# Attention values, their copies and exponentials by pairs of units, and batch 3's first steps two slots later

## What is computed

```
x = x + ssm(layernorm(x))          # conv, SiLU, decay/drive, scan over time, projection
x = x + ffn(layernorm(x))          # 8 experts of 512, all of them for each token
x = x + attention(layernorm(x))    # 16 heads of 8
x = x + ffn(layernorm(x))          # the same ffn again

# ffn
g = einsum('bsh,ehf->ebsf', x, w_gate);  u = einsum('bsh,ehf->ebsf', x, w_up)
h = silu(g) * u
out = einsum('ebsh,bse->bsh', einsum('ebsf,efh->ebsh', h, w_down), cw)

# attention: a row sees its own chunk of 10 and 25 tokens to the left
scores = einsum('bhsd,bhtd->bhst', q, k) + mask
out = einsum('bhst,bhtd->bhsd', softmax(scores), v)
```

## Time and profile before

| | us |
|---|---|
| median of 3 runs | 1425.51 (1422.82 to 1425.74) |
| profiled execution, its own time | 1425.63 |
| its span, first to last instruction | 1423.8 |
| PE busy | 1364.1 |
| DVE, ACT, POOL busy | 951.1, 773.1, 517.1 |

### The profile page before, as it was taken

How to read it: one execution, slowest core, us unless ns; L and a number is a source line. 1 busy time by engine, 2 the same in 40 slices (tenths; PEclk the granted TensorE clock), 3 DMA queues, 4 the chain that set the end, 5 groups by cost and what they waited for, 6 DMA issues and landing times.

```text
span 1423.8 us, 31460 instructions
## 1 busy us (share of the span) xinstructions
PE 1364.1 (96%) x12700; PEld 1179.9 (83%) x12700; DVE 951.1 (67%) x2294; ACT 773.1 (54%) x1049; POOL 517.1 (36%) x517
## 2 busy tenths in 40 slices
PE   4889999999999999999999989999999999999998
PEld 3788777888888888887888878888888888888887
DVE  6766777775876668568675676757856675576543
ACT  6565648653565556637475665556634563365321
POOL 4260564533423453247312751236503421341000
PEclk9999999999999999999999999999999999999999
DMA  6210231003010310131003300050003000300000
GB/s 233 59 31 17 67 79 32 20 12 78 2 47 16 71 24 1 47 68 35 9 2 83 64 2 9 1 116 32 2 1 73 8 2 1 71 9 2 9 1 8
DMA packets 70235, 51.39 MB, mean 36 GB/s; under 512 B 4140, under 2 KB 60508, under 8 KB 70092
## 3 DMA queue, kind: packets, MB, share of 16 engines
q1 hardware_dynamic: 70060, 49.38, 14.4%
q10 hardware_dynamic: 32, 0.02, 0.0%
HBM read 44.92 MB, written 4.46 MB: 35 GB/s over the span
## 4 chain that ended last, share of the span: by engine, by line
PE 79%; DVE 8%; POOL 5%; issue 4%; ACT 3%; DMA 0%; DVEq 0%; POOLq 0%
PE pd L1125 26%; PE pg L289 8%; PE pu L289 7%; PE pg L291 7%; PE pg L290 7%; PE pu L290 7%; PE pu L291 7%; PE att_ps L766 2%; POOL arena L713 2%; PE att_ps L791 2%; DVE h L1234 1%; POOL arena L715 1%; PE pd L1117 1%; DVE x L1222 1%; PE side_ps L326 1%
## 5 line engine op out<-in xcount | busy, mean ns | idle before, releaser
L1185 ACT ACTIVATE h<-pg 128x512 f32<-128x512 f32 x512 | 304.3, 598 | 601.8 <-PE pg L291 599.6
L1125 PEld LDWEIGHTS pd<-w_down,h 128*128 128x128 f32 x3840 | 483.4, 192 | 33.9 <-issue 4.1
L1125 PE MATMUL pd<-w_down,h 128*128 128x128 f32 x3840 | 489.7, 276 | 1.3 <-DVE x L1222 1.1
L1234 DVE TENSOR_TENSOR h<-h,pu 128x512 f32<-128x512 f32 x512 | 344.8, 678 | 214.9 <-PE pu L291 204.8
L289 PE MATMUL pg<-ffn_x_hi,w_gate_hi 128*128 128x512 f32 (+1 forms) x544 | 248.3, 456 | 1.1 <-DVE ffn_x_lo L376 1.1
L289 PE MATMUL pu<-ffn_x_hi,w_up_hi 128*128 128x512 f32 (+1 forms) x544 | 210.3, 387 | 12.6 <-DVE h L1234 12.5
L290 PE MATMUL pu<-ffn_x_lo,w_up_hi 128*128 128x512 f32 (+1 forms) x544 | 208.4, 383 | 0.0
L291 PE MATMUL pg<-ffn_x_hi,w_gate_lo 128*128 128x512 f32 (+1 forms) x544 | 208.3, 383 | 0.0
L290 PE MATMUL pg<-ffn_x_lo,w_gate_hi 128*128 128x512 f32 (+1 forms) x544 | 208.2, 383 | 0.0
L291 PE MATMUL pu<-ffn_x_hi,w_up_lo 128*128 128x512 f32 (+1 forms) x544 | 207.9, 382 | 0.0
L976 POOL TENSOR_TENSOR att_arena<-att_arena,r_sums 128x512 f32<-128x512 f32 (+1 forms) x72 | 72.6, 1008 | 272.9 <-DVE r_sums L856 272.8
(11 more groups left out here) (222 smaller groups left out, 1440.1 us busy)
## 6 DMA issues: line engine op xcount, KB each, us to landing
arena<-bc_spread SPq DMA_DIRECT2D x56, 256.0 KB, 4.6
att_arena<-v_rows SPq DMA_DIRECT2D x64, 144.0 KB, 3.9
att_arena<-v_rows SPq DMA_DIRECT2D x64, 128.0 KB, 3.7
arena<-in_x SPq DMA_DIRECT2D x8, 256.0 KB, 3.1
x<-in_x SPq DMA_DIRECT2D x8, 256.0 KB, 3.5
w_down<-in_w_down SPq DMA_DIRECT2D x8, 256.0 KB, 5.0
v_rows<-att_arena SPq DMA_DIRECT2D x8, 256.0 KB, 2.3
out<-x SPq DMA_DIRECT2D x8, 256.0 KB, 2.2
```

What stands on the lines that cost most here:

```text
L1125: last = nc.tensor.matmul(pd[:, t * P:(t + 1) * P], h_b[:, d % NH, t * P:(t + 1) * P], wd[:, d % NCH, :], start=d % CPE == 0 and t == 0, s ...
L1185: nc.scalar.activation(h_b[:, c % NH, :], pg[c % 2][:, :], ACT.Silu).then_inc(gate_done, 1)
L1234: nc.vector.tensor_tensor(h, h, pu[d % 2][:, :], ALU.mult).then_inc(h_done, 1)
```

## The change

The attention of a batch goes by pairs of units from the exponentials on. A new function `Att.pair(j, n, part)` gives the slot of a step: the pair's first unit plus a part of its own for even and odd units; in the last pair, of one unit, the part is scaled by 0.75.

- PE: `values(m)` has all windows of a pair in one block, in one bank, and stands behind the scores of the next pair.
- ACT: one Exp over 1024 columns for a pair.
- DVE: masks, maxima, sums and transposes are still one for each unit, but both units' follow one another or lie close; the copy to `attT` is one for a pair, 120 columns instead of 60. `smax` and `rsum` get a second buffer.
- POOL: subtractions and multiplications likewise; `like_heads` does parts 0, 1 in pair 0 and parts 2, 3 in pair 1.
- Batch 3's `st`, `rows`, `ln` and `win` are two slots later; batch 1's `y` moves from 23.1 to 23.5.

```diff
-        return dict(st=-25.2, rows=-24.2, ln=-22, win=0.7, dt=7.7, k=(10.7, 13.7, 16.4, 19.1), y=23.1)
+        return dict(st=-25.2, rows=-24.2, ln=-22, win=0.7, dt=7.7, k=(10.7, 13.7, 16.4, 19.1), y=23.5)
...
-    return dict(st=o - 11, rows=o - 9.5, ln=o - 9, win=o - 6.5, dt=o + 1, k=(o + 10, o + 16, o + 26, o + 32), y=o + 42)
+    s = 2 if i == 3 else 0
+    return dict(st=o - 11 + s, rows=o - 9.5 + s, ln=o - 9 + s, win=o - 6.5 + s, dt=o + 1, k=(o + 10, o + 16, o + 26, o + 32), y=o + 42)
...
-S_SC, S_MASK, S_MASK1, S_MAX, S_SUM, S_TURN, S_VAL, S_OUT, S_Q = 1 / 8, 1 / 4, 5 / 8, 3 / 8, 1 / 8, 5 / 8, 7 / 8, 1, 3 / 8
+S_SC, S_MASK, S_MAX, S_SUB, S_EXP, S_SUM, S_NORM, S_TURN, S_VAL, S_OUT, S_Q = \
+    -0.125, (0.25, 0.25), (0.5, 0.625), (0.625, 0.875), 1.125, (1.5, 1.5), (1.375, 1.375), (1.875, 2.125), 2.75, 2.875, 0.25
+S_LAST = 0.75
...
+            def pair(j, n, part):
+
+                part = part[n % 2] if isinstance(part, tuple) else part
+                return Att.at(j, n // 2 * 2 + (part if n + 1 < NUNIT else S_LAST * part))
...
-                    for i, w in enumerate(UNITS[n]):
+                    pe.wait_ge(p_t, NUNIT * j + min(2 * m + 2, NUNIT))
+
+                    for i, w in enumerate(PAIRS[m]):
...
+                for m in range(NPAIR):
+                    yield Att.pair(j, 2 * m, S_SC)
+                    if m == 0:
+                        ab.wait_free(pe, ("k", j))
+                    scores(m)
+                    if m:
+                        yield Att.pair(j, 2 * m - 2, S_VAL)
+                        values(m - 1)
...
-                for n in range(NUNIT):
-                    yield at(n + 3 / 4)
-                    act.wait_ge(s_sub, NUNIT * j + n + 1)
-                    u = s_u[n % 2][:, 0:len(UNITS[n]), :, :]
+                for m in range(NPAIR):
+                    yield Att.pair(j, 2 * m, S_EXP)
+                    act.wait_ge(s_sub, NUNIT * j + min(2 * m + 2, NUNIT))
+                    u = att_ar[:, 0:len(PAIRS[m]) * 4 * WK]
                     nc.scalar.activation(u, u, ACT.Exp, scale=float(HD) ** -0.5).then_inc(s_exp, 1)
...
-                    for part in {0: (0, 1), 2: (2,), 3: (3,)}.get(n, ()):
-                        yield Att.at(j, n + 3 / 4 + part % 2 / 8)
+                    for n in units:
+                        yield Att.pair(j, n, S_SUB)
+                        less_maxima(n)
+                    for part in {0: (0, 1), 1: (2, 3)}.get(m, ()):
+                        yield Att.pair(j, 2 * m, 0.9 + part % 2 / 8)
                         like_heads(part)
```

More of the change, by code:

```diff
@@ L170, in build @@
         o1 += L
-        rsum = sb("r_sums", [P, 2, 4])
-        smax, = (att_ar[:, o1 + 8 * i:o1 + 8 * i + 8].rearrange("p (w g) -> p w g", w=2) for i in range(1))
+        rsum = sb("r_sums", [P, 2, 2, 4])
+        smax = [att_ar[:, o1 + 8 * i:o1 + 8 * i + 8].rearrange("p (w g) -> p w g", w=2) for i in range(2)]
         xn_att = att_ar[:, 0:L].rearrange("p (t d) -> p t d", t=TT)
@@ L772, in scores, with values @@
                                         ab.fill(last, ("s", j, m, b))
-                yield at(S_SC)
-                ab.wait_free(pe, ("k", j))
-                scores(0)
-                for n in range(NUNIT):
[L778 to L784, removed]
+                def values(m):
+                    pe.wait_ge(v_set, 4 * j + min(m + 1, 4))
+                    name = ("o", j, m)
                     ps = ab.take(pe, name)
-                    pe.wait_ge(p_t, NUNIT * j + n + 1)
-                    for i, w in enumerate(UNITS[n]):
+                    pe.wait_ge(p_t, NUNIT * j + min(2 * m + 2, NUNIT))
+                    for i, w in enumerate(PAIRS[m]):
                         for v in range(2):
@@ L863, in turned @@
                     if n >= 2:
-                        ab.wait(dve, ("o", j, n - 2))
+                        ab.wait(dve, ("o", j, n // 2 - 1))
                     nc.vector.transpose(pt_flat[:, n % 2, 0:nw * 4 * WK],
                                         u.rearrange("p w g k -> p (w g k)")).then_inc(p_t, 1)
-                for n in range(NUNIT + 1):
-                    if n:
-                        yield at(n + S_SUM)
-                        sums(n - 1)
-                    if n < NUNIT:
-                        yield at(n + S_MAX)
-                        maxima(n)
-                    if n:
-                        yield at(n + S_TURN)
-                        turned(n - 1)
+                for m in range(NPAIR):
+                    units = range(2 * m, min(2 * m + 2, NUNIT))
+                    for n in units:
+                        yield Att.pair(j, n, S_MAX)
+                        maxima(n)
+                    for n in units:
+                        yield Att.pair(j, n, S_SUM)
+                        sums(n)
+                    for n in units:
+                        yield Att.pair(j, n, S_TURN)
+                        turned(n)
                 yield Att.end(j) + 2.5
@@ L907, in dve_out @@
             def dve_out(dve, link, j):
[L908 to L911 removed]
+                for m in range(NPAIR):
+                    yield Att.pair(j, 2 * m, S_OUT)
+                    nw, name = len(PAIRS[m]), ("o", j, m)
+                    nq = WQ if nw > 1 else QW
                     ab.wait(dve, name)
                     ps = ab.ps(name)[:, 0:nw * QW].rearrange("p (w q) -> p w q", q=QW)[:, :, 0:nq]
[L914 removed]
+                    to = attT[:, 4 * m * WQ:4 * m * WQ + nw * nq].rearrange("p (w q) -> p w q", q=nq)
                     ab.free(nc.vector.tensor_copy(to, ps), name)
@@ L931, in sp @@
                         if j:
-                            ab.wait(sp, ("o", j - 1, NUNIT - 1))
+                            ab.wait(sp, ("o", j - 1, NPAIR - 1))
                     else:
```

64 lines of the change are left out of this document (31 added, 33 removed).

## The result

The changed kernel took **1415.58 us** (median of 4, 1414.36 to 1416.32) against 1425.45 us for the kernel before in the same comparison: a ratio of 0.9934, 95% interval 0.9917 to 0.9951. The forecast was 1413 us, range 1403 to 1425. The profiled execution took 1414.36 us, with a span of 1412.6 us, 11.2 us shorter than the span of before.

The account below looks back on a forecast made before the run. TensorE was taken to bound the kernel, busy 1364.1 of 1423.8 us. Blocks -9.6, stalls going -11.2, stalls coming +6.9 and batch 3 +1.2 sum to -12.7 us: 1413 us, range 1403 to 1425.

Parts of the forecast that it names:

- Blocks, 9.6 us: On PE, merging two blocks of values saves one entry and exit, 0.30 us a pair, 9.6 us in all.
- Rival B: On PE, the block entry price is not saved: 1423 us, or 1428 at the scores' pace; chance 0.10.
- Exponentials: On ACT, 32 exponentials of 1024 columns and 195 table loads; busy time falls from 773 to about 704 us, nothing counted directly.
- Stalls that go, 11.2 us: Three long PE waits give 5.5 us, clock falls behind them 5.1, values' wait for masks 0.6.
- (1): Score matmuls' 1.97 us wait at 834.55 goes, because scores precede the previous pair's values and copies lie earlier.
- (2): Routing matmuls' 2.05 us wait at 820.61 for `ffn_x_lo` shrinks to some 0.8, the attention exponential coming after the copies.
- (3): Transposes' 2.56 us wait at 385.43 for the convolution shrinks to 0.4, a value part moving three chunks ahead.
- Stalls that come, 6.9 us: Consecutive POOL value parts hold DVE at five places, 1.03 us each, plus one clock fall of 1.7 us.
- Batch 3, 1.2 us: Moving batch 3's first steps adds waits of 1.0 us at W_in and 1.4 at routing, less 1.20 that goes.
- Rival A: Paired bursts on DVE and POOL cost more than the late moments they replace: 1434 us; chance 0.12.
- D: The pairs' chain exceeds its slots, so PE waits at each of 32 larger values blocks: 1429 us; chance 0.06.
- C: The waits go and none comes: -22 us, 1404 us; chance 0.14.

Follow-up runs that it names:

- values split: Changed kernel with each pair's values on PE in two blocks of two windows, one chunk apart, same bank; 1424.63 us, ratio 0.9992 to the kernel before.
- adjacent pair: Changed kernel with a pair's two exponentials separate again, one right behind the other; 1416.05 us, ratio 0.9943 to the kernel before.
- parts paired: Kernel before with only value part 3 moved right behind part 2 on POOL, in unit 2; 1427.22 us, ratio 1.0009 to the kernel before.
- parts apart: Changed kernel with value part 3 masked on POOL in pair 2 instead of right behind part 2 in pair 1; 1412.83 us, ratio 0.9907.
- parts tiny: Changed kernel with POOL's masking cut to 32 elements of each value part, the rest left unmasked; 1406.32 us, ratio 0.9868 to the kernel before.
- parts apart but in batch 5: Changed kernel with value part 3 in pair 2, except batch 5's attention, which keeps the changed kernel's order; 1411.65 us, ratio 0.9909.

## Why the prediction came out as it did

**Blocks, 9.6 us.** Right in mechanism, the term was too large: 8.3 us by the rows, 8.0 by the run with the values split. The step that was off is the "16 more matmuls are 0.13 us", carried on in a straight line: it holds from 16 to 32, but 32 more matmuls move the next start by 0.69 - 0.39 = 0.30 us, not 0.26. Rival B (the entry price not saved, or the pace of the scores) is excluded.

**Exponentials.** The 704 us came as worked out (702.1), and the wording "I count nothing for it directly" was right for the merged instruction but for the wrong reason. I had looked at whether ACT keeps up with the SiLUs. What decides is DVE, which takes its sums in order: had the pairs kept the exponentials a chunk apart, the whole gain would have been lost (10.7 us). The change avoids this by having them in one place. My expectation for that run missed as well; the adjacent pair showed the reason. The prediction's own room for the SiLU did not add up either: a chunk and a half is 1.5 x 2.29 = 3.4 us, so a hold of 3.6 does not fit "with a few tenths to spare". It did little harm: PE waits for a SiLU once, 0.44 us at 948.50.

**Stalls that go, 11.2 us.** (1) The score matmuls' wait near 834 went, but not for the reason given: 1.36 of its 1.97 us go by the value part's move alone, with the order of scores, values and copies as before. (2) The routing wait near 820 went entirely (0.8 us had been left for it): at 815.96 those matmuls wait for nothing. The run with the parts paired shows that the parts have no share in it, and ScalarE's order that the exponential's place has. (3) The transposes' wait near 387 kept 1.17 us, not 0.4: the convolution is late there even with the parts cut to almost nothing, when the wait is 1.16 us all the same. Together 2.0 + 2.05 + 1.4 = 5.4 us for 5.5. The half-clock places behind all three are gone, as said. The same move of the exponential that freed the copies near 820 put one ahead of them in a later pass: there the routing matmuls wait 1.04 us at 1155.27, which was not foreseen.

**Stalls that come, 6.9 us.** The mechanism is shown by the runs with the parts apart or tiny; the sum was about right, and the places were not. Of five named, the scan of batch 4's attention cost 2.27 us and that of batch 5's 0.45 us (two waits beside it, 0.44 and 0.34, stay with the parts tiny). The three others cost PE nothing: at batch 0's two no wait of size stands, and batch 7's mix step, though held on DVE, has no PE wait behind it. The largest cluster, 1.95 us at 375.88 and 0.33 just before it, was not named: I had gone through DVE's order for places that already had a scan or a mix, and passed over batch 4's LayerNorm rows. The known wait near 651 stayed at 1.1 us. That makes 2.27 + 0.45 + 1.95 + 0.33 = 5.0 us in waits for the 5.2 that were forecast: near by luck, since only two of the five places count in it.

**Batch 3, 1.2 us.** The two waits are 0.79 (1.0 said) and 2.02 (1.4), less the 1.20 that went: 1.6 us. Behind the second, the clock fell (217.3), which the sum had not at this place. Against the order of before the term was near; as a judgement of the move it had the wrong sign, since unmoved the pairs have 1.6 us more idle time.

**The sum.** Without the blocks my terms came to -3.1 us. The span moved by 11.2 us, of which the blocks are 8.3, so -2.9: one new half-clock place and three gone, as forecast in number (-2 x 1.7), and waits that cancel. So the forecast of 12.7 missed the span by 1.5 us, nearly all of it the size of the block term. By the medians the gain is 9.9 us and the forecast 2.6 us too fast; half of that is that the profiled execution, 1414.36 us, was the fastest of the four. That the waits cancel is in part luck. Some 3 us went that the sum did not have (0.98 at 264.56, 0.67 at 998.33, 1.1 near 958 to 975, 0.40 at 730.41 in the kernel before), and some 3 us came that it did not have and that stay with the parts tiny (0.73 at 556, 0.88 at 794, 0.44 at 948.50, 1.04 at 1155). The sign given in its last part, "open idle falls from 27.5 to some 20", contradicted the sum: its own terms (6.1 us of waits going, 5.2 + 1.2 coming) gave 27.8, and 27.4 was measured. The slip was to count the clock's 5.1 us as idle time, whereas PE is busy in it. Rival A did not happen (no wait recurs in each pair), nor D; C's 22 us would have needed the parts to be free, and the run with tiny parts, 1406, is what comes near it.

## What to carry to other kernels

Count how often the tensor engine changes between tile shapes: each block of small matmuls here cost 0.25 to 0.30 us beside its work, and two blocks made one gave most of the gain, while the waits that were taken away came back elsewhere. When steps of two units are brought together on one engine, bring the producers together as well, since an in-order consumer stands still for the later one. And a long GpSimd instruction has to be placed by what VectorE does beside it and by what is queued behind it, for each batch by itself: the same slot is free in one and costs 2 us in another.

## What the runs showed of the hardware that I had not expected

**A four-column instruction can be held as long as a large one.** The timeline of POOL and VectorE in batch 7's attention of the changed kernel, two value parts and an addition beside the second:

```profile
1243.29 4.17 POOL L983 TENSOR_TENSOR att_arena<-att_arena,pack 128x1024 f32<-128x1024 f32 x2
...
1245.26 2.22 DVE L393 TENSOR_TENSOR mix_sums<-mix_sums 128x4 f32<-128x4 f32 x1
```

The addition of four columns took 2.22 us, longer than one value part (4.17 / 2), and ended when the second part did (1247.48 and 1247.46). So here a held instruction waited for the whole of the other engine's instruction, although it is tiny itself. The Trainium skill, SBUF — State Buffer, "SBUF: two separate sides", has this rule (the port pair is locked, the loser blocks fully), and the size of the effect on so small an instruction, and the 12.3 us that DVE lost to 32 value parts, are what the runs add.

**The clock falls at places that one stall does not determine.** In the changed kernel PE waited 3.36 us at 106.51 and the clock stayed at full (1.00 from 106 to 112), then fell at 160; in the run with the parts apart but in batch 5, PE waited 3.27 us at 106.59 and the clock was 0.50 over the same 6 us, and did not fall at 160. The work there is the same in both. Near 376 it is alike: before the same transposes PE waits 1.95 us in the changed kernel and with the values split, and only in the second is the clock at half behind it (378). And it differs between executions of one kernel: of 23 executions of the kernel before on one chip, 12 had a mean granted clock of 0.990 and took 1426.6 to 1428.6 us, 6 had 0.992 and 1424.9 to 1425.6, and 4 had 0.993 and 1423.4 to 1423.7. So a single half-clock place in one profiled execution says nothing about a change, and differences of 2 to 3 us between two kernels can be clock alone.
